# A chain of four attention layers on one core: the norms' subtraction and product moved from VectorE to GpSimd, and one constant of the scan's schedule changed

## The reference, cut to what matters

```python
# L0: self attention with a mask, 16 heads of 16; a gated context term; feed-forward of 1024
t = x + attn(layer_norm(x, g1, be1), mask) @ Wo.T + bo + ctx @ Wg.T + bg
x = t + relu(layer_norm(t, g2, be2) @ W1.T + b1) @ W2.T + b2
# L1: norms of ctx and x, one-head attention, an MLP of width 4, a norm, self attention
# L2: causal attention with 16 heads, residual, layer norm, feed-forward with gelu
# L3: attention with 8 heads of 32, norms, then a scan over the tokens
def step(s, u_t):
    s = silu(s @ A.T) + u_t
    return (s, s)
_, states = scan(step, zeros, U)          # here 128 tokens, 16 batches, 64 states
out = residual + states @ Cmat + mod
```

## Time and profile before

| | us |
|---|---|
| three timed executions, median | 802.48 (801.19 to 804.74) |
| the profiled execution | 803.27 |
| its span | 801.4 |
| PE busy in the span | 762.5 |
| DVE busy | 570.5 |
| ACT busy | 437.3 |
| POOL busy | 336.8 |

### The profile page before, as it was taken

The page is one execution under the profiler, slowest core; times in us unless marked ns, Lnnn a source line. Parts: engine busy times, 40 slices in busy tenths (PEclk is TensorE's granted clock), DMA queues, the critical chain, the costliest instruction groups (busy, mean ns, idle before and its releaser), DMA issues.

```text
span 801.4 us, 17323 instructions
## 1 busy us (share of the span) xinstructions
PE 762.5 (95%) x5964; PEld 608.4 (76%) x5964; DVE 570.5 (71%) x2307; ACT 437.3 (55%) x1771; POOL 336.8 (42%) x356
## 2 busy tenths in 40 slices
PE   7799989999999999998999999999999889899998
PEld 5587878788788878887888788878887667655665
DVE  3868888868968995899579987896788467541121
ACT  2655666476835683577456826784366275442321
POOL 1716454535644564344526563455354543330000
PEclk9999998999999999999999999999999999999975
DMA  9810001000000000000000000000000000002012
GB/s 344 280 54 1 22 1 48 27 0 2 20 15 0 2 21 15 1 2 14 21 1 2 14 15 0 2 2 2 1 2 1 1 1 2 1 8 59 22 34 52
DMA packets 17897, 22.33 MB, mean 28 GB/s; under 512 B 4109, under 2 KB 14482, under 8 KB 17170
## 3 DMA queue, kind: packets, MB, share of 16 engines
q1 hardware_dynamic: 16232, 19.78, 8.0%
q10 hardware_dynamic: 1578, 1.45, 0.6%
HBM read 17.82 MB, written 2.10 MB: 25 GB/s over the span
## 4 chain that ended last, share of the span: by engine, by line
PE 71%; DVE 14%; issue 4%; SPq 4%; POOL 3%; ACT 3%; DMA 0%; DVEq 0%; POOLq 0%
PE work_bank L659 20%; PE work_bank L668 16%; PE work_bank L922 7%; PE scores_bank L831 4%; PE scores_bank L707 3%; PE work_bank L651 3%; PE work_bank L742 3%; PE work_bank L629 3%; DVE probsT L1242 2%; DVE probs L1137 2%; DVE xn L1155 2%; ACT probs L1375 2%; SPq L556 2%; SPq L528 1%; PE work_bank L786 1%
## 5 line engine op out<-in xcount | busy, mean ns | idle before, releaser
L1004 POOL TENSOR_TENSOR probs<-probs,rtotal 128x512 f32<-128x512 f32 (+1 forms) x164 | 165.8, 1024 | 209.7 <-DVE rtotal L1231 209.4
L1375 ACT ACTIVATE probs<-probs,nmx 128x128 f32<-128x128 f32 x512 | 198.0, 390 | 72.7 <-DVE nmx L1137 72.4
L1242 DVE COPY probsT<-work_bank 128x512 f32<-128x512 f32 (+1 forms) x164 | 106.6, 665 | 17.3 <-PE work_bank L922 16.8
L668 PE MATMUL work_bank<-L_w,hidden 128*128 128x256 f32 x512 | 113.6, 380 | 0.0
L668 PEld LDWEIGHTS work_bank<-L_w,hidden 128*128 128x128 f32 x512 | 96.1, 190 | 12.8 <-ACT hidden L1427 0.2
L922 PE MATMUL work_bank<-ident,probs 128*128 128x128 f32 x640 | 92.8, 280 | 5.2 <-POOL probs L1004 3.4
L1375 ACT ACTIVATION_READ_ACCUMULATOR probs<-probs,nmx 128x1 f32 x512 | 96.8, 189 | 0.0
L922 PEld LDWEIGHTS work_bank<-ident,probs 128*128 128x128 f32 x640 | 72.7, 142 | 24.3 <-POOL probs L1004 11.3
L1004 POOL TENSOR_TENSOR rstd<-veps,half 128x2 f32<-128x2 f32 (+1 forms) x59 | 40.7, 689 | 115.3 <-DVE veps L1188 115.1
L1137 DVE CUSTOM_DVE_ANT_0 probs<-scores_bank,bias 128x128 f32<-128x128 f32 x256 | 56.9, 284 | 11.0 <-PE scores_bank L707 10.7
L659 PE MATMUL work_bank<-B_actT,L_w 128*128 128x256 f32 (+1 forms) x288 | 60.7, 359 | 1.0 <-DVE B_actT L1205 1.0
(11 more groups left out here) (196 smaller groups left out, 1487.3 us busy)
## 6 DMA issues: line engine op xcount, KB each, us to landing
L_w<-in_L_w SPq DMA_DIRECT2D x4, 1024.0 KB, 14.8
x_all<-in_x SPq DMA_DIRECT2D x8, 256.0 KB, 4.1
cT<-in_ctxT SPq DMA_DIRECT2D x7, 256.0 KB, 2.6
c_in<-in_ctx SPq DMA_DIRECT2D x7, 256.0 KB, 2.7
rows<-in_rows SPq DMA_DIRECT2D x1, 1280.0 KB, 9.7
out<-x_all SPq DMA_DIRECT2D x8, 128.0 KB
bias<-in_mask SPq DMA_DIRECT2D x7, 128.0 KB, 2.1
L_wk<-in_L_wk SPq DMA_DIRECT2D x3, 256.0 KB, 6.5
```

The lines of the kernel that those rows point to most:

```text
L668: mm = nc.tensor.matmul(d[:, b * D:b * D + D], xT, w, start=(n == 0), stop=(n == len(todo) - 1))
L1004: return nc.gpsimd.tensor_tensor(out, a0, a1, op)
L1242: nc.vector.tensor_copy(turn_slot(s, i, key)[:, 0:n], d[:, 0:n * P].rearrange("p (j k) -> p j k", j=n))\
L1375: ins = nc.scalar.activation(e_at[slot][:, j, :], src, ACT.Exp, bias=nmx[:, slot, j:j + 1], scale=1.0 if s == "C" else -1.0, accum_out=tot ...
```

## The change

- All 67 `norm` jobs leave VECTOR_ORDER. POOL's job `rstd` now does them: after the power it waits for its own result (`link`), for the slot's last user, and then issues one tensor_scalar (subtract, multiply) per block.
- `xn` has four slots instead of three, taken in the order of POOL's `rstd` jobs. GPSIMD_ORDER, TENSOR_ORDER and SCALAR_ORDER are as before.
- DVE gets waits on `normed` where it could overwrite what POOL still reads: at `stat` (the moments' slot four back), at A's `out`, and at the halved `out` of C.
- SECOND_FROM goes from 100 to 99.

```diff
 VECTOR_ORDER = """
-H0.stat.x H0.norm.x H0.flip.x G0.stat.c G0.bias A0.max.0 A0.max.1 A0.max.2 A0.max.3 A0.rec.0 H1.stat.x A0.rec.1 H0.v
+H0.stat.x H0.flip.x G0.stat.c G0.bias A0.max.0 A0.max.1 A0.max.2 A0.max.3 A0.rec.0 H1.stat.x A0.rec.1 H0.v
...
-PROBS, TURNED, NORMED, MOMENTS = 6, 6, 3, 4
+PROBS, TURNED, NORMED, MOMENTS = 6, 6, 4, 4
...
-STATED, NORM_AT = count("d", "stat"), count("d", "norm")
-RSTD = count("g", "rstd")
+STATED, NORM_AT = count("d", "stat"), count("g", "rstd")
...
-NORMS = [x for x in program("d") if x[2][0] == "norm"]
+STATS = [x for x in program("d") if x[2][0] == "stat"]
+NORMS = [x for x in program("g") if x[2][0] == "rstd"]
...
-FIRST_FROM, SECOND_FROM, THIRD_FROM = 67, 100, 122
+FIRST_FROM, SECOND_FROM, THIRD_FROM = 67, 99, 122
...
@@ POOL, job rstd
-                    add(to[:, of], veps[:, n, of], half[:, of], ALU.pow).then_inc(rstd_ready, 1)
+                    links += 1
+                    link(add(to[:, of], veps[:, n, of], half[:, of], ALU.pow), links)
+                    at = NORM_AT[s, i, step] - 1
+                    if at >= NORMED:
+                        t, j, (_, before) = NORMS[at - NORMED]
+                        pool.wait_ge(*filled_at(t, j, "flip", "cn" if before == "c" else before))
+                        if before in ("x3", "x5"):
+                            pool.wait_ge(*summed_at(t, j, before + "b"))
+                        elif before == "cr":
+                            pool.wait_ge(*summed_at(t, j, "crg"))
+                    src, _ = norm_io(s, i, key)
+                    for b in blocks(s, i):
+                        nc.gpsimd.tensor_scalar(norm_slot(s, i, key)[:, b, :], src[:, b, :], moments[:, n, b, 0:1],
+                                                to[:, b:b + 1], ALU.subtract, ALU.mult).then_inc(normed, 1)
...
@@ DVE, job stat
+                    at = STATED[s, i, ("stat", key)] - 1
+                    if at >= MOMENTS:
+                        t, j, (_, before) = STATS[at - MOMENTS]
+                        dve.wait_ge(*normed_at(j, t, before))
...
-                elif kind == "norm":
-                    normalise(s, i, key)
...
@@ DVE, job out of A
                     dve.wait_ge(*summed_at("A", i, "xb"))
+                    dve.wait_ge(*normed_at(i, "G", "c"))
+                    if i:
+                        dve.wait_ge(*normed_at(i - 1, "M", "x3"))
...
@@ DVE, job out of C
+                    if kind == "out" and halved(s, i):
+                        dve.wait_ge(*normed_at(NT - 1, "M", "x3"))
```

More of the change, by code:

```diff
@@ L116 @@
 M2.rec.a C0.rec.0 A3.rec.6 H4.flip.x B1.flip.o C0.rec.1 A3.turn.7 B1.stat.x5 A3.turn.5 M2.turn.a A3.turn.6
[L117 to L120, removed]
+ J2.v C0.rec.2 A3.mix.1 C0.max.3 B1.flip.x5 C0.turn.0 C0.rec.3 G4.bias H4.v C0.turn.2 C0.turn.1 C0.turn.3
@@ L145 @@
-C3.turn.3 H7.v C3.turn.2 B4.flip.x5 M5.stat.cr C3.mix G7.bias M5.norm.cr G6.stat.c G6.norm.c M5.flip.cr A6.out.1
-A6.out.0 C3.out M5.max.s M5.rec.s C3.stat.x7 A6.stat.x2 A7.max.0 A6.norm.x2 C3.norm.x7 A7.rec.0 A7.max.1 A7.max.2
+B4.flip.o C3.rec.2 J5.v C3.rec.1 A6.turn.6 C3.rec.3 A6.turn.7 C3.turn.0 B4.stat.x5 A6.mix.1 C3.turn.1
+C3.turn.3 H7.v C3.turn.2 B4.flip.x5 M5.stat.cr C3.mix G7.bias G6.stat.c M5.flip.cr A6.out.1
+A6.out.0 C3.out M5.max.s M5.rec.s C3.stat.x7 A6.stat.x2 A7.max.0 A7.rec.0 A7.max.1 A7.max.2
@@ L156 @@
-A7.ffn1.2 C5.norm.x6 B6.max.0 B6.max.1 B6.max.2 B6.max.3 B6.rec.0 A7.ffn1.1 B6.rec.1 A7.ffn1.0 A7.ffn1.3 B6.max.4
+A7.turn.6 A7.turn.7 C4.rec.2 J6.v C4.turn.0 C4.max.3 A7.mix.1 B5.flip.x5 C4.rec.3 C4.turn.2 C4.turn.1
+M6.stat.cr C4.turn.3 C4.mix G7.stat.c C4.out M6.flip.cr A7.out.0 C4.stat.x7 A7.out.1 A7.stat.x2
+M6.max.s M6.rec.s M6.turn.s B5.ffn2 C4.flip.x7 M6.self A7.flip.x2 C4.drive C5.stat.x6
+A7.ffn1.2 B6.max.0 B6.max.1 B6.max.2 B6.max.3 B6.rec.0 A7.ffn1.1 B6.rec.1 A7.ffn1.0 A7.ffn1.3 B6.max.4
@@ L161 @@
[L161 to L162 removed]
+C5.turn.1 C5.rec.3 B6.stat.x5 C5.turn.2 C5.turn.0 C5.turn.3 B6.flip.x5 C5.mix M7.stat.cr
+C5.out C5.stat.x7 M7.flip.cr M7.max.s M7.rec.s C5.flip.x7 B6.ffn2 C6.stat.x6 M7.turn.s C5.drive
+ M7.self C6.flip.x6 C6.max.0 C6.max.1 J7.v C6.rec.0 C6.max.2 C6.max.3 C6.rec.1 C6.rec.2 C6.rec.3 B7.max.0
@@ L167 @@
+B8.rec.1 C6.out B8.rec.0 B7.flip.x5 B8.rec.2 C6.stat.x7 B8.rec.3 B8.turn.0 C6.flip.x7 B8.turn.1 B7.ffn2
+B8.turn.2 B8.turn.3 C7.stat.x6 B8.mix.0 C6.drive B8.flip.o C7.flip.x6 B8.stat.x5 B8.flip.x5
 C7.max.0 C7.max.1 C7.max.2 C7.rec.0 C7.max.3 C7.turn.0 C7.rec.2 C7.rec.1 C7.rec.3 B8.ffn2 C8.stat.x6 C7.turn.1
-C7.turn.3 C8.norm.x6 C7.turn.2 C8.flip.x6 C7.mix C7.out C7.stat.x7 C8.max.0 C8.max.1 C8.max.2 C7.norm.x7 C8.max.3
+C7.turn.3 C7.turn.2 C8.flip.x6 C7.mix C7.out C7.stat.x7 C8.max.0 C8.max.1 C8.max.2 C8.max.3
@@ L169 @@
 C8.rec.0 C7.flip.x7 C7.drive C8.rec.2 C8.rec.3 C8.rec.1 C8.turn.1 C8.turn.2 C8.turn.0 C8.turn.3 C8.mix C8.out
-C8.stat.x7 C8.norm.x7 C8.flip.x7 C8.drive
+C8.stat.x7 C8.flip.x7 C8.drive
 """
```

98 lines of the change are left out of this document (38 added, 60 removed).

## The result

The changed kernel takes 891.08 us (median of 4, 889.18 to 892.04) beside 803.61 us for the kernel before on the same chip (median of 4, 801.19 to 805.11): a ratio of 1.109 [1.105, 1.113]. The forecast was 786 with a range of 777 to 798. Executions of some of these kernels fall into two groups some 40 to 50 us apart, by the clock of the scan; the four here are all of the slow one, and a ratio with an interval leaves that group out where a kernel has both.

What follows compares the result with a forecast made beforehand. PE, busy 762.5 of 801.4 us, bounds the kernel, by its lateness and clock. From 803.3 us, 10.9 for SECOND_FROM and 6 for DVE's relief come off: 786.4, median 786; range 780 to 791, 8 in 10 within 777 to 798.

Steps and rivals of the forecast that it cites:

- The price of a norm on POOL: POOL's moved tensor_scalar was taken as 0.50 us, between a memset's 0.24 us and two-input operations at 612 and 728 ns.
- the upper row: POOL's dearer two-input operation of 128x256 in the profile before, 728 ns, taken as above a norm's price.
- the sum: Profiled 803.3 us less 10.9 for SECOND_FROM and 6 for DVE's relief: 786.4, for a median of 786.
- rival C: POOL becomes what PE waits for, slower than before; gains used up at about 0.95 us a norm; chance 0.07.
- Who is late: Attention products behind POOL's longer roots: 50 of 180 start later, 9 end after PE took them, together 3.7 us.
- the walk: POOL's timeline with each root lengthened, idle time absorbing it: 3.7 us late at 0.50 a norm, 14 at 0.82.
- the clock term of step 99: Scan steps 100 to 127 at 0.57 us each if the clock stays at 1.00: 9.4 us saved.
- What DVE gives back: PE's waits for DVE, 12.0 us in sum, less 3.9 for POOL's lateness leaves 8.1, of which 6 counted.
- the two gaps that I named: PE's idle gaps of 2.65 us near 115 us and 2.61 us near 360, predicted to shrink below 1 us.
- SECOND_FROM: Moving it to 99 removes the gap at scan step 99: 0.6 + 9.4 + 0.9 = 10.9 us if the clock holds.
- The clock at the start of the scan: Scan clock read as 1.00 from 721 to 769.2 us in the profile before; no loss priced there.
- Rival A: The clock falls anyway, by another cause or new gap, so SECOND_FROM wins only 0.6 us: 796.7 us; chance 0.17.

Runs made afterwards that it cites:

- experiment 4: The changed kernel with each norm on POOL writing only 64 of its 256 columns, the rest a constant: 787.36 us, ratio 0.981.
- experiment 6: The changed kernel with each norm on POOL writing only 128 of its 256 columns: 799.46 us once, and 847.42, 850.12 and 848.56.
- experiment 1: The kernel before with SECOND_FROM = 99 and nothing else of the change: 793.87 us, ratio 0.987.
- experiment 2: The changed kernel with SECOND_FROM back at 100, so the norms on POOL alone: 851.98, 853.58 and 852.64 us, and 892.59 once.
- experiment 13: The changed kernel with seven dense matmuls replacing the filler of scan step 30: 840.41, 841.04, 844.12 us, and 858.94, 860.29, 863.16.
- experiment 12: The changed kernel with 24 dense matmuls in front of C7's drive, ahead of the scan: 849.77 us once, five runs at 899.31 to 902.35.

## Why the prediction was wrong

**The price of a norm on POOL: the step that failed.** "A norm has one tensor input and two scalars per partition, so it lies between": it does not. It takes 1.22 us, 1.7 times the upper row that I took as a bound and 2.4 times the 0.50 of the sum. Those rows were of other operations, and nothing in the trace made them one. The root itself was the hint, 0.70 us for two columns; I saw it under rival C and gave it 0.07. With norms of 0.58 us the kernel takes 787 us, near the 786 of the forecast, though with three quarters of the norms' columns left out.

**Who is late: right, at the wrong price.** That products behind the root would hold up PE, and how it grows with the price, came out as the walk has it (experiments 4 and 6). Rival C named the mechanism, and its signs came (a norm above 0.8 us, turns that wait over 15 us for `probs`). It put the point of no gain at 0.8 us with the clock term of step 99 left out and at 0.95 with it; like for like the starts of the scan give some 0.7, and some 0.85 with the 10.6 us of experiment 1 (0.80 + 0.42 x (708.4 + 10.6 - 714.45) / 40.7, an estimate). At 1.22 us C's sum, with the walk's 56.0, is 803.3 - 10.9 - 12.0 + 56.0 = 836, beside 838 to 842 for the runs in which the scan kept its clock. The walk counted as waiting what is partly pace, so the agreement is better than the account.

**What DVE gives back: right in size, not in kind.** I counted 6 us net, nearly all of it waits; with norms of 0.58 us the scan starts 6.4 us ahead of experiment 1 and 4.5 ahead of the profiled run of before. But PE's idle time ahead of it is 34.8 us, and it was 34.4 before and 34.7 in experiment 1. What the waits for DVE gave, the waits for POOL took: 8.4 and 2.2 us where there were 3.4 and none. The 4.5 us are PE's busy time, 669.2 instead of 674.0, at a mean clock of 1.00 instead of 0.99. In one execution of each that can be the luck of the falls as well as the move. One of the two gaps that I named stayed: the 2.65 us for DVE's `probsT` is one of 2.5 us in the changed kernel, where no norm stands in DVE's queue any more. The other, of 2.61 us at 362.74, has gone from PE's waits for DVE. DVE was busy 504.7 us, where I had 490.

**SECOND_FROM: right, and not visible in the result.** Alone it is worth 10.6 us in the scan against 10.9 forecast, and 1.3% of the kernel. The 0.56 us gap does bring the clock down (experiments 1 and 2). In the changed kernel the clock was down already 3 us ahead of step 1 (752 against 755.18), so nothing was left for it to save.

**The clock at the start of the scan: the second step that failed.** The sum took 1.00 up to step 99 as given, and so put at nothing what a fall ahead of the scan costs. I had read the gap of 1.3 us ahead of the flip at 698.7 us and the clock of 1.00 behind it, and did not ask what the same gap does in another run, or one closer to the scan. Rival A let the clock fall anyway, but priced only the part from step 100 on; none of the rivals has a scan that starts with the clock down. It adds 39.2 us in the profiled run, and 49.8 against a scan that keeps its clock (132.2 less 82.4): as much as the price of the norms.

The Trainium skill ("TensorE: Matmul & The Clock Gate", Why this matters for your kernels) ties the fall to idle gaps far longer than these. Here falls came behind 0.56 and 1.39 us, and the measurement decides. The Trainium skill ("GPSIMD Engine Reference", Engine selection) calls one-input work on GpSimd "roughly line-rate". The one-input norm took three times DVE's 0.41 us, and twice the time of a two-input product of its size on POOL, 1.22 against 0.61 us.

**What stays open.** Why the same gap is followed by a fall in one run and not in the next, in equal programs. With gaps of 1.2 to 1.5 us ahead of it the scan began with the clock down, by the times, in seven of eight runs of the changed kernel, in one of four of experiment 2 and in three of six of experiment 13. These differ only from step 99 and from step 30 on, and ran on different chips; 11 of 18 together are no more than a rough chance. Nor is it shown why the clock fell in the scan's first steps in experiments 6 and 12. Nor was it tried whether norms split between DVE and POOL, one block each, would pay.

## What to carry to other kernels

Rows of other operations on the same engine are no bound for one that moves: measure the form itself first. Here 27 instructions behind the last work of a kernel gave nine prices in one run. Price the in-order queue behind the moved work, not the engine's busy share: POOL at 55% cost more than DVE at 71%. A serial stretch with thin matmuls mostly kept the clock that it started with; cover the idle times just ahead of it and inside it, and put a few dense matmuls into it as insurance (7 matmuls, some 3 us at full clock, gave back 30 of the 50 here, from step 30 on). The version that is faster than both kernels is the constant alone: 793.87 us, 0.987 [0.983, 0.990] of before.

## What the runs showed of the hardware

- POOL tensor_scalar in fp32 with two operations and scalars per partition: 0.58, 0.80, 1.22 and 2.07 us for 64, 128, 256 and 512 columns. Constants in place of the scalars save 0.14 us, one operation less 0.2 to 0.3. The subtraction and product as two tensor_tensor instructions with broadcast scalars would take 2 x 0.61 by estimate, the same; that was not run.
- The clock came down from 1.00 to 0.50 behind idle times of PE from 0.56 to 2.21 us, and in experiments 6 and 12 in the scan's first steps, where the last 4 us had no more than 0.47 us of idle time in two pieces; behind the same idle times it also held (1.26 us at 698 in before). In dense parts it was back after some 3 us (746:749); in the scan it stayed at 0.50 for over 120 us, and came back in a dense block and, once, behind four matmuls of 128x256. With equal programs the times lie 50 us apart, so a kernel with such a stretch wants eight runs or more, not three.
